# Reordered waits, clears and weight loads at the stage boundaries, and a second result bank for the late shared tiles, in a one-core attention and mixture-of-experts kernel

## What is computed

```python
# attention: 16 query heads, 4 key/value heads of 128; keys and values of context and tokens
q = rope(rms_norm(layernorm(x) @ Wq.T)); k = rope(rms_norm(kv_in @ Wk.T)); v = kv_in @ Wv.T
x = x + tanh(g_xattn) * (softmax(q @ k.T * SCALE) @ v) @ Wo.T
# experts: 8, two for each token, and a shared one of width 352
y = layernorm(x)
top_v, top_i = top_k(softmax(y @ w_router), 2)            # weights normalised to 1
routed = 2.5 * sum_j top_v[j] * (silu(y @ w_gate[i_j]) * (y @ w_up[i_j])) @ w_down[i_j]
shared = (silu(y @ ws_gate) * (y @ ws_up)) @ ws_down
x = x + tanh(g_ffn) * (routed + shared)
```

## Time and profile before

| | |
|---|---|
| median of 3 runs | 1284.08 us (1283.68 to 1286.13) |
| profiled execution: its own time | 1284.96 us |
| its span, first to last instruction | 1283.2 us |
| mean granted TensorE clock | 0.989 of full |
| busy: PE, PEld | 1210.8 us (94%), 1150.5 us (90%) |
| busy: DVE, POOL, ACT | 1039.7 us (81%), 949.3 us (74%), 878.6 us (68%) |
| chain that ended last | PE 85%, DVE 9%, ACT 2%, issue, DMA and POOL 1% each |

### The profile page before, as it was taken

The page is one execution under the profiler, slowest core; times in us unless marked ns, Lnnn a source line. Parts: engine busy times, 40 slices in busy tenths (PEclk is TensorE's granted clock), DMA queues, the critical chain, the costliest instruction groups (busy, mean ns, idle before and its releaser), DMA issues.

```text
span 1283.2 us, 31482 instructions
## 1 busy us (share of the span) xinstructions
PE 1210.8 (94%) x8825; PEld 1150.5 (90%) x8826; DVE 1039.7 (81%) x3015; ACT 878.6 (68%) x3745; POOL 949.3 (74%) x1143
## 2 busy tenths in 40 slices
PE   0399999999999999999999999999999889999998
PEld 0389999999999999999999999999999789999898
DVE  8878888888888888888888888888888477777444
ACT  3577777777777777777777777777777336666322
POOL 7577888888887888888888887888887215556554
PEclk9799999999999999999999999999999899999999
DMA  5512222223333322222323333222235826554574
GB/s 191 169 34 72 87 92 86 90 86 110 93 102 106 96 86 86 86 90 90 95 94 112 104 98 123 90 72 72 76 105 177 274 72 188 165 165 149 174 238 141
DMA packets 127093, 148.78 MB, mean 116 GB/s; under 512 B 13760, under 2 KB 107328, under 8 KB 126016
## 3 DMA queue, kind: packets, MB, share of 16 engines
q1 hardware_dynamic: 112192, 126.10, 32.4%
q0 software_dynamic: 6528, 17.90, 3.7%
q10 hardware_dynamic: 8320, 4.19, 1.1%
HBM read 67.26 MB, written 80.89 MB: 115 GB/s over the span
## 4 chain that ended last, share of the span: by engine, by line
PE 85%; DVE 9%; ACT 2%; issue 1%; DMA 1%; POOL 1%; SPq 0%; ACTq 0%; DVEq 0%; POOLq 0%
PE b_o L1651 13%; PE b_kv L1600 13%; PE b_q L1586 12%; PE b_sc L1625 8%; PE b_aT L1640 8%; PE b_pT L1633 5%; PE b_qT L1614 4%; PE b_q L1829 3%; PE b_kv L1829 3%; PE b_aT L1761 3%; PE b_q L1743 2%; PE b_kT L1610 2%; PE b_sc L1743 2%; DVE sincos L413 1%; ACT probs L939 1%
## 5 line engine op out<-in xcount | busy, mean ns | idle before, releaser
L1600 PE MATMUL b_kv<-w_group,kv_in_hi 128*128 128x256 f32 x1024 | 213.5, 306 | 9.8 <-DVE k_sin L1187 9.8
L1586 PE MATMUL b_q<-w_group,kv_in_hi 128*128 128x512 f32 x512 | 173.3, 420 | 31.9 <-DVE kv_in_lo L1173 29.3
L1600 PEld LDWEIGHTS b_kv<-w_group,kv_in_hi 128*128 128x128 f32 x1024 | 168.7, 192 | 17.4 <-DVE k_sin L1187 10.5
L722 POOL TENSOR_TENSOR qk_r<-qk_me,minus_half 128x6 f32<-128x6 f32 x128 | 174.3, 1361 | 10.0
L939 ACT ACTIVATE probs<-b_sc,neg_max 128x128 f32<-128x128 f32 x512 | 180.1, 371 | 1.5 <-DVE neg_max L1211 1.5
L726 POOL TENSOR_TENSOR q_rot<-q_rot,q_sin 128x512 f32<-128x512 f32 x128 | 164.3, 1283 | 9.7 <-DVE q_sin L1201 4.8
L1651 PE MATMUL b_o<-wo_hi,aT_hi 128*128 128x256 f32 x512 | 154.3, 301 | 0.5 <-DVE aT_lo L1225 0.2
L933 ACT ACTIVATE pT<-b_pT 128x512 f32<-128x512 f32 x128 | 76.6, 599 | 112.6 <-PE b_pT L1633 110.7
L1600 PE MATMUL b_kv<-w_group,kv_in_lo 128*128 128x256 f32 x512 | 145.0, 283 | 0.0
L1651 PE MATMUL b_o<-wo_lo,aT_hi 128*128 128x256 f32 x512 | 143.0, 279 | 0.0
L1651 PE MATMUL b_o<-wo_hi,aT_lo 128*128 128x256 f32 x512 | 143.0, 279 | 0.0
(11 more groups left out here) (252 smaller groups left out, 3966.1 us busy)
## 6 DMA issues: line engine op xcount, KB each, us to landing
xs_scratch<-zeros SPq DMA_DIRECT2D x34, 1032.0 KB, 6.3
s_in<-xs_scratch SPq DMA_DIRECT2D x72, 129.0 KB
yT_scratch<-yT SPq DMA_DIRECT2D x32, 256.0 KB, 2.0
yS<-yT_scratch SPq DMA_DIRECT2D x32, 256.0 KB, 3.6
routed<-ys_scratch SPq DMA_DIRECT2D x32, 256.0 KB, 3.6
w_hi_all<-w_scratch SPq DMA_DIRECT2D x3, 1536.0 KB, 8.7
x_in<-in_x SPq DMA_DIRECT2D x32, 128.0 KB, 2.4
ctx_raw<-in_ctxT SPq DMA_DIRECT2D x32, 128.0 KB, 2.6
```

Of the source, the lines that this page charges most:

```text
L722: nc.gpsimd.tensor_tensor(qk_r[g % 2][:], qk_me[:], minus_half[:, 0:REP + NB], ALU.pow).then_inc(r_ready, 1)
L1586: last = nc.tensor.matmul(b_q[:], kv_in[p][a][:, c, 1:3, :], wq_of(b, gg)[:, c, :], start=(c == 0 and (a, b) == PASSES[0]), stop=(c == DC ...
L1600: last = nc.tensor.matmul(b_kv[:, s * 2 * HD:(s + 1) * 2 * HD], kv_in[p][a][:, c, 2 * s:2 * s + 2, :], wkv_of(b, c)[:, g % KVH, :], start= ...
```

## The change

SyncE clears the rows of a tile in that tile and not in the next, and the spare rows at the start; in the last tile it issues all four quarters of the weights before the store of yT. POOL waits for a scatter only before the next one, sums the keys before these waits, takes the second layer norm's power and the sine table ahead of the scatters, has a new place for one of the waits ahead of the cosine table, and writes out two pairs instead of one before its loop. ACT runs an empty Silu before the last `probs_out`. VectorE finds the slots' limits by a comparison of expert numbers and one reduction in place of three rounds of shifted adds, and the first row of a slot from one weighted sum. The first slot's transpose and gate product move ahead of the last early tile's down product. The late tiles have two result banks, b_aT and b_o, in turn, so that `add_shared(t - 2)` stands behind `hidden(t)`.

```diff
-        b_late = b_q, b_sc, b_pT, b_aT
+        b_late = (b_q, b_sc, b_pT, b_aT), (b_q, b_sc, b_pT, b_o)
-            return b_early[t % 2] if t < EARLY else b_late
+            return b_early[t % 2] if t < EARLY else b_late[t % 2]
...
-                need(sp, st_zero[p], 16 * i)
+                need(sp, st_zero[p], 16 * (i + p))
...
-                    if not (first and p == 0):
-                        clear_rows(t - 1, i - 1 + p, 1 - p)
+                        clear_rows(0, 0, 0)
+                        sp.dma_start(xs_dram[E * STRIDE:, :].rearrange("(a p) n -> p a n", p=P),
+                                     zeros[:].unsqueeze(1).to_broadcast([P, SPARE, XW])).then_inc(st_zero[1], 16)
+                    if isinstance(i, int) and i == 1 and p == 0:
+                        clear_rows(1, 0, 1)
+                    if not first:
+                        clear_rows(t, i, p)
                     if last and p == 1:
+                        clear_rows(TILES, PAIRS, 0)
                         for g in range(2):
                             load_hi(g)
                     if not (first and p == 0):
                         store_x1(t - 1, 1 - p)
+                    if last and p == 1:
+                        for g in range(2, KVH):
+                            load_hi(g)
+                    if not (first and p == 0):
                         store_yT(t - 1, 1 - p)
...
-            for g in range(2, KVH):
-                load_hi(g)
...
-            clear_rows(TILES - 1, PAIRS - 1, 1)
-            clear_rows(TILES, PAIRS, 0)
...
                         scales(n + 1, g + 1)
                         query_sum(n + 1, g + 1)
-                        if g == 1 and not first:
-                            need(pool, row_ready, t - 1)
-                            pool.wait_ge(st_zero[p], 16 * (i if isinstance(i, int) else i))
-                        if g == 2 and not first:
-                            need(pool, st_xs, 32 * (t - 2) + 16)
-                        if g == 3 and not first:
-                            need(pool, st_xs, 32 * (t - 1))
                         key_sum(n + 1, g + 1)
+                    if g == 0 and not end:
+                        need(pool, st_xs, 32 * (t - 2))
+                        cos_table(i + p, 1 - p)
+                        layer_rstd(t + 1, 1 - p)
+                    if g == 1 and not first:
+                        need(pool, row_ready, t - 1)
+                        need(pool, st_zero[p], 16 * (i + p))
+                        if end:
+                            need(pool, st_xs, 32 * (t - 2))
+                    if g == 2 and not first:
+                        need(pool, st_xs, 32 * (t - 2) + 16)
+                    if g == 1 and not (first and p == 0):
+                        layer_rstd2(t - 1)
+                    if g == 2 and not end:
+                        sin_table(1 - p)
                     if g in (1, 2) and not first:
                         scatter(t - 2, p, g - 1)
-                    if g == 0 and not end:
-                        cos_table(i + p, 1 - p)
-                        layer_rstd(t + 1, 1 - p)
-                    if g == 2 and not end:
-                        sin_table(1 - p)
-                    if g == 1 and not (first and p == 0):
-                        layer_rstd2(t - 1)
...
-            walk(pool, pair)
+            walk(pool, pair, start=2)
...
+            nc.scalar.activation(gates_raw[:, 0:1], gates[:, 0:1], ACT.Silu)
             probs_out(4 * TILES - 1, 3)
...
-            hidden_hi(EARLY - 1)
...
             slot_hi(0, 0)
+            hidden_hi(EARLY - 1)
             slot_hi(1, 1)
...
+            nc.vector.tensor_tensor(below_e[:], expert_no[:].unsqueeze(1).to_broadcast(by_expert),
+                                    expert_no[:].unsqueeze(2).to_broadcast(by_expert), ALU.is_le)
...
-            then(V.tensor_copy(upto[0][:], full[:]))
-            for n, d in enumerate((1, 2, 4)):
-                V.tensor_copy(upto[n + 1][:, 0:d], upto[n][:, 0:d])
-                then(V.tensor_tensor(upto[n + 1][:, d:E], upto[n][:, d:E], upto[n][:, 0:E - d], ALU.add))
+            V.tensor_scalar(worth[:], full[:], -float(P), float(STRIDE), ALU.mult, ALU.add)
+            then(V.tensor_tensor(upto_w[:], below_e[:], full[:].unsqueeze(1).to_broadcast(by_expert), ALU.mult))
+            then(V.tensor_reduce(upto[:], upto_w[:], AX.X, ALU.add))
...
-            then(V.tensor_scalar(s_b[:], s_expert[:], float(STRIDE), None, ALU.mult))
-            then(V.tensor_tensor(s_a[:], slot_no[:], s_first[:], ALU.subtract))
-            then(V.scalar_tensor_tensor(out=s_row[:], in0=s_a[:], scalar=float(P), in1=s_b[:], op0=ALU.mult, op1=ALU.add))
             V.tensor_scalar(slot_expert[:], s_expert[:], float(E - 1), None, ALU.min)
+            then(V.scalar_tensor_tensor(out=s_row[:], in0=slot_no[:], scalar=float(P), in1=s_first[:], op0=ALU.mult,
+                                        op1=ALU.add))
...
             slot_lo(0, 0)
             slot_dest(0, 0)
-            add_shared(EARLY - 1)
...
+            add_shared(EARLY - 2)
+            hidden_lo(EARLY - 1)
             slot_lo(1, 1)
             slot_dest(1, 0)
+            add_shared(EARLY - 1)
...
             for t in range(EARLY, TILES):
                 hidden(t)
-                if t > EARLY:
-                    add_shared(t - 1)
+                if t > EARLY + 1:
+                    add_shared(t - 2)
                 hidden_lo(t)
+            add_shared(TILES - 2)
             add_shared(TILES - 1)
...
-                need(pe, shared_ready, t)
+                need(pe, shared_ready, t if t < EARLY else t - 1)
...
             slot_T(0, 0)
-            shared_down(EARLY - 1)
-            slot_T(0, 1)
+            shared_down(EARLY - 2)
+            shared_hidden_T(EARLY - 1)
...
                     slot_gate_up(m, p, expert[q])
+                    if first and q == 0:
+                        pe.wait_ge(hT_lo, EARLY)
+                        slot_T(0, 1)
+                        shared_down(EARLY - 1)
```

More of the change, by code:

```diff
@@ L250, in flamingo @@
         full = sb("full", [P, E], F32, late_at)
-        upto = [sb(f"upto{n}", [P, E], F32, late_at) for n in range(4)]
+        upto = sb("upto", [P, E], F32, late_at)
+        worth = sb("worth", [P, E], F32, late_at)
         slot_no = sb("slot_no", [P, SLOTS], F32, late_at)
         nowhere = sb("nowhere", [P, MANY], F32, late_at)
-        s_expert, s_first, s_row, s_a, s_b = [sb(n, [P, SLOTS], F32, x_res_at) for n in (
-            "s_expert", "s_first", "s_row", "s_a", "s_b")]
+        s_expert, s_first, s_row = [sb(n, [P, SLOTS], F32, x_res_at) for n in ("s_expert", "s_first", "s_row")]
+        below_e, upto_w = [sb(n, [P, E, E], F32, x_res_at) for n in ("below_e", "upto_w")]
         assert x_res_at[0] <= x_res_end
@@ L824, in _ @@
             pool.wait_ge(row_ready, T1 + 1)
-            pool.wait_ge(st_zero[1], 16 * PAIRS)
+            pool.wait_ge(st_zero[1], 16 * (PAIRS + 1))
             for j in range(TOPK):
@@ L1485, in _ @@
             then(V.tensor_tensor(past[:], slot_no[:].unsqueeze(2).to_broadcast(by_slot),
-                                 upto[3][:].unsqueeze(1).to_broadcast(by_slot), ALU.is_ge))
-            V.tensor_tensor(past_w[:], past[:], full[:].unsqueeze(1).to_broadcast(by_slot), ALU.mult)
+                                 upto[:].unsqueeze(1).to_broadcast(by_slot), ALU.is_ge))
+            V.tensor_tensor(past_w[:], past[:], worth[:].unsqueeze(1).to_broadcast(by_slot), ALU.mult)
             then(V.tensor_reduce(s_expert[:], past[:], AX.X, ALU.add))
@@ L1501, in _ @@
                 hidden_lo(t - 1)
-            add_shared(EARLY - 2)
-            for p in range(2):
-                for o in (P, P + AGAIN):
-                    V.memset(s_hid[p][:, o + REST:o + AGAIN], 0.0)
-            hidden_lo(EARLY - 1)
             def slot_lo(m, p):
@@ L1540, in _ @@
             slot_dest(0, 0)
-            add_shared(EARLY - 1)
+            for p in range(2):
+                for o in (P, P + AGAIN):
+                    V.memset(s_hid[p][:, o + REST:o + AGAIN], 0.0)
+            add_shared(EARLY - 2)
+            hidden_lo(EARLY - 1)
             slot_lo(1, 1)
             slot_dest(1, 0)
+            add_shared(EARLY - 1)
             def slots(k, first, last):
```

7 lines of the change are left out of this document (2 added, 5 removed).

## The result

The changed kernel takes 1296.88 us (median of 4 runs, 1296.39 to 1298.13), the kernel before 1283.88 beside it: ratio 1.0099, 95% interval 1.0082 to 1.0117. It is slower by 1%; the forecast was 1275.6, with 0.17 for slower.

The account below looks back on a forecast made before the run. The prediction took TensorE to bound attention, so gains had to come from its waits elsewhere. Its terms, -4.1 - 1.0 - 1.2 - 4.45 + 5.8 - 3.5 = -8.45 us, gave 1275.6 us on the median, range 1268 to 1288.

Parts of the forecast that it names:

- weights and clock: Between attention and the first shared tiles: earlier weight loads save 2.15 us of TensorE waiting, a full clock 2.0; together -4.1 us.
- slot table: In the early shared tiles: fewer small dependent VectorE operations ahead of two TensorE waits for hidden halves; -1.0 us.
- woven slots: At the last early tile: the first slot's transpose and gate product fill TensorE's wait of 0.96 us; -1.2 us.
- banks: In the late tiles: a second result bank removes TensorE's 2.65 us wait and 1.8 us of low clock; -4.45 us.
- The clears: In attention tiles: SyncE's clears, issued a tile sooner, stay hidden behind the tile's own loads; 0 us.
- the key transposes' first wait: In attention step g=2: TensorE waits for POOL's late key sum, taken as 0.2 us in each of tiles 2 to 30.
- POOL's order: In attention: the power ahead of the scatter leaves POOL idle for the variance and late into g=2; +5.8 us.
- the block of the key sum: In attention step g=2: POOL's product and VectorE's normalising block each other, so the key sum gives another 0.31 us.
- My rival for this: In attention: POOL's lateness also reaches g=3, making a second key sum late, 9.0 us on top of 7.0; 1289.3, chance 0.14.
- the tie: In attention: POOL's cosine product starts just before VectorE's L1219 and delays it in 12 tiles; half gone, -3.5 us.
- The blocked scatter: In attention: the scatter is held beside VectorE's normalising of y, 0.54 us in 29 tiles, 15.7; 1291.3, chance 0.03.

## Why the prediction was wrong

**What was right.** Behind attention the steps of the sum came out: weights and clock -5.3 (forecast: -5.55, less 1.4 that POOL's lateness takes in the last tile; that lateness measured 1.5 at the last keys and 1.0 at the attended values), slot table -0.95 (-1.0), woven slots -1.15 (-1.2), banks -4.54 in the profile (-4.45). The clears cost nothing, the stores slipped by a tile without harm. The slot table, the woven slots and the empty Silu were never run by themselves; their figures are differences between the two profiles. Of the key transposes' first wait I had the place, the cause (idle for the variance, 1.40) and the lateness (entry to g=2 1.2 us later).

**The step that failed: POOL's order, +5.8.** It was mis-sized twice.
- The stall in g=2 is 0.33 a tile, not 0.2. I had the block of the key sum (0.31), but the chain from scale to key sum took another 0.12 (713.27 to 718.34 is 5.07 in tile 21, and in all 29 tiles on average; 4.64 in the earlier trace rows plus 0.31 is 4.95). That is 9.7 instead of 5.8.
- The lateness is carried on to g=3: 5.9 us more. My rival for this had 0.14, with the words "Against: POOL has idle time in g=3". The rows show that it lies behind the key sum (2.54) and only 0.27 and 0.18 ahead of it. The trace of the kernel before has these rows. What neither the forecast nor the rival had is the partner: in tiles 2 to 25 the sine product now lies beside VectorE's split of a weight piece and takes up to 1.61 us. Without it, in tiles 26 to 30, a lateness of 1.0 us stalls nothing in g=3. The run with the sine product in the idle wait agrees, where that lateness is 0.1 to 0.5 and the product meets no split.

In the terms of that rival the forecast was 7.0 + 9.0 in attention; 9.7 + 5.9 came. That its second figure is near is partly luck: it stood for 29 tiles with one block of 0.31 each. Its total of 1289.3 was short by the tie, the first tile, the slots and the end.

**The tie, -3.5.** No ties were lost; there were 14 long steps instead of 11, +1.05 in g=1, and 0.8 in g=0. Over all kernels of this study the long steps number from 0 to 17. Half of them gone was a guess with nothing under it; as good a value was 0.

**In no term of the sum:** the low clock in the first tile (1.7) and the stop in the slots (1.85). Each is in some kernels' profiles and not in others', whatever their edits, the kernel before with the banks alone having both. With one profile for each kernel it stays open whether they belong to a kernel or to a single execution; the changed kernel's profiled execution was the fastest of its four.

**The end, +1.7.** This is a cost of the change that I didn't have. The span ends 4.3 to 4.7 us after VectorE's last instruction in all 11 kernels that put the additions off to the end, and 2.7 in the 7 that don't, the two with two banks and caught-up additions among them. So it is the late additions, not the banks. What passes in these 1.7 us no trace shows; that stays open.

So the sum, against the profiled execution: forecast -8.45, measured +11.4 in the span. The 19.9 between them are 3.9 + 5.9 for the two stalls, 4.6 for the ties, 0.8 in g=0, and 5.2 for first tile, slots and end; what is left, -0.5, is mostly in the last tile.

**The banks' 4.45** hold only where the clock falls. With one bank the wait is 2.65 to 2.9 in five profiles; the clock fell to half behind it in two of them (before, and the one with SyncE's part alone: 17.6 and 17.9 us over four tiles) and stayed full in three (16.1). Less the 1.7 at the end, the banks as the change has them are worth 1 to 1.5 us at full clock. The run with the banks alone agrees: nothing that can be told.

**The blocked scatter** (0.03) isn't seen. In the changed kernel the scatter at 712.18 lies across VectorE's L1256 and takes 1.06, as does the one at 720.09, which has no such neighbour. The 29 of this kind average 1.07, the others 1.06. The rule of the Trainium skill that the prediction weighed ("SBUF — State Buffer", "SBUF: two separate sides") is on VectorE in a two-port mode. No run shows whether L1256 runs in one, and in all 29 tiles the scatter had begun before it, so the trace doesn't test the rule. Longer scatters stand beside VectorE instructions with two operands in SBUF: beside L1317, in the run with only the sine product put back, 24 scatters take 1.29 to 1.47.

## What to carry to other kernels

An instruction that waits for another engine, moved ahead of one that waits for nothing, makes all that stands behind it late by its whole idle time. Before pricing it, list for every step behind it how much idle time the engine has *ahead of its due work*, row by row; the engine's total idle time says nothing, since most of it may lie behind the last due result. And where two engines block each other, moving one instruction by some tenths may only change the partner: look up what will lie beside it in its new place, try the order, and trust no count of lucky ties.

## What the runs showed of the hardware

- Two elementwise instructions, one of POOL and one of VectorE with two operands in SBUF, exclude each other whole in the rows above. Where POOL's product starts first, it runs at its own length (0.99 to 1.02 us) and VectorE's ends after it: L1301 took 0.81 for 0.16, L1225 1.37 for 0.56. Where VectorE's starts first, POOL's is held: the key sum beside L1225 took 1.05 for 0.72, the sine product beside L1317 1.61 for 1.0. One row is otherwise: L1317 at 681.01 starts 0.27 us before the sine product, while a scatter still runs, and is the one held (1.95 for 0.78). The Trainium skill says the same in the section named above ("exclusive lock, not a bandwidth split"); that it reaches down to an instruction on two columns (L1301) is what I hadn't expected.
- A scatter issued by POOL takes 1.06 us of its time with no such neighbour, and 1.29 to 1.47 beside VectorE's L1317.
- The same wait of TensorE, 2.65 to 2.9 us at the same place, was followed by a granted clock of 0.50 in two of five profiles and by 1.00 in three. A wait of 1.70 was followed by 0.50 in one profile (SyncE's part alone, from 1034 us) and by 1.00 in the kernel before.
- In 9 of the 18 profiles the slots take 1.9 to 2.0 us longer, always between the 57th and the 59th of the 72. In the changed kernel's profile ScalarE and VectorE stop there while POOL and TensorE go on. It stands in kernels of both families and no single edit goes with it; what they wait for the trace doesn't name.
